# The normalised context in the expert layer transposed by block pairs on all 128 partitions, each tile stored as four pieces

## What is computed

```python
x = x + _L0_xattn_ref(_layernorm(x, axis=-1), ctx_512, ...)
x = x + _L0_ffn_ref(_layernorm(x, axis=-1), ...)   # 8 experts, all computed, weighted by the top 2
...
# _L0_ffn_ref
x1 = jnp.einsum('bsh,ehf->bsef', x, W1) + b1
x2 = jnp.einsum('bsh,ehf->bsef', x, W2) + b2
z = x1 * x2
g = jnp.einsum('bsef,efg->bseg', z, Wg) + bg
o = g * jax.nn.sigmoid(g) * (jnp.einsum('bsef,efg->bseg', z, Wl) + bl)
y = jnp.einsum('bsef,efh->bseh', o, W3) + b3
...
# layer 3, attention a2: the context is normalised over its 64 columns
yn = _ln(y, lny_g, lny_b)
```

## Time and profile before

| | us |
|---|---|
| median of 3 runs | 4445.98 (4444.93 to 4448.55) |
| the profiled execution, its own time | 4435.46 |
| its span in the profile | 4433.6 |
| share of the span: PE / DVE / ACT / POOL busy | 92% / 78% / 62% / 61% |

### The profile page before, as it was taken

One profiled execution on the slowest core, in us unless ns is written; L12 is line 12 of the kernel. 1 busy time (PEld: TensorE's weight loads), 2 busy tenths in 40 slices (PEclk: granted clock), 3 DMA queues, 4 the chain that ended last, 5 costly groups with the idle time before them and its releaser, 6 DMA issues. The chain is left out here.

```text
span 4433.6 us, 102799 instructions
## 1 busy us (share of the span) xinstructions
PE 4082.9 (92%) x40217; PEld 2922.3 (66%) x40217; DVE 3436.2 (78%) x6755; ACT 2732.0 (62%) x5298; POOL 2695.9 (61%) x2421
## 2 busy tenths in 40 slices
PE   7999999889988999999699999995996899999967
PEld 4777777655555777777557777774664577777754
DVE  6999998567778888888688888875554888888842
ACT  5777777534436777777467777771441677777721
POOL 3888788646674777777447777772002476777720
PEclk9999999889998999999699999995997999999975
DMA  4333333113331111111011111100000111111000
GB/s 113 90 94 94 89 95 89 47 62 114 112 98 58 54 37 54 39 52 38 19 44 53 37 54 45 45 30 18 1 1 28 43 46 45 50 49 45 30 12 9
DMA packets 107229, 236.66 MB, mean 53 GB/s; under 512 B 13496, under 2 KB 43464, under 8 KB 105368
## 3 DMA queue, kind: packets, MB, share of 16 engines
q1 hardware_dynamic: 106296, 230.03, 17.7%
q10 hardware_dynamic: 448, 0.06, 0.0%
HBM read 164.87 MB, written 50.26 MB: 49 GB/s over the span
## 5 line engine op out<-in xcount | busy, mean ns | idle before, releaser
L466 POOL TENSOR_TENSOR wst<-wst 125x384 bf16<-125x384 f32 (+1 forms) x1536 | 1632.6, 1063 | 833.0 <-ACT wst L664 768.3
L664 ACT ACTIVATE wst<-ps 125x448 f32<-125x448 f32 x3072 | 1498.5, 543 | 408.1 <-PE ps L164 399.1
L721 DVE TENSOR_TENSOR wst<-wst 125x512 bf16<-125x512 f32 (+1 forms) x1536 | 1404.0, 915 | 269.7 <-ACT wst L664 254.5
L164 PE MATMUL ps<-big,cx 128*125 128x448 bf16 (+1 forms) x6144 | 1435.5, 355 | 0.0
L164 PEld LDWEIGHTS ps<-cx,wst 125*128 125x128 bf16 x23040 | 1105.4, 98 | 354.4 <-issue 60.5
L164 PE MATMUL ps<-cx,wst 125*128 125x65 bf16 (+2 forms) x23040 | 1202.3, 204 | 27.5 <-POOL wst L466 13.3
L164 PEld LDWEIGHTS ps<-big,cx 128*125 128x125 bf16 (+1 forms) x6144 | 814.6, 137 | 287.4 <-issue 23.0
L164 PE MATMUL ps<-cx,big 128*128 128x500 bf16 (+1 forms) x2688 | 713.3, 318 | 27.8 <-DVE wst L691 15.0
L688 DVE CUSTOM_DVE_ANT_0 wst<-ps,wst 128x500 bf16<-128x500 f32 x896 | 603.7, 674 | 162.0 <-PE ps L164 122.8
L613 ACT ACTIVATE wst<-ps 128x500 bf16<-128x500 f32 x896 | 531.1, 593 | 221.9 <-PE ps L164 174.3
L691 DVE TENSOR_REDUCE wst<-ps 128x1 f32<-128x500 f32 x896 | 600.3, 670 | 36.1 <-PE ps L164 26.8
(11 more groups left out here) (203 smaller groups left out, 4232.7 us busy)
## 6 DMA issues: line engine op xcount, KB each, us to landing
cx<-ctxT SPq DMA_DIRECT2D x96, 375.0 KB, 3.5
cx<-ctxN SPq DMA_DIRECT2D x64, 377.9 KB
cx<-in_ctxN SPq DMA_DIRECT2D x64, 375.0 KB
cx<-ctxT SPq DMA_DIRECT2D x96, 187.5 KB, 3.8
ctxN<-cx SPq DMA_DIRECT2D x32, 377.9 KB
ynN<-cx SPq DMA_DIRECT2D x32, 377.9 KB
cx<-ynN SPq DMA_DIRECT2D x32, 377.9 KB
cTs<-in_ctxT SPq DMA_DIRECT2D x64, 187.5 KB, 6.8
```

Of the source, the lines that this page charges most:

```text
L164: return t.matmul(o, l, r, start=start, stop=stop, skip_group_check=True)
L466: g.tensor_tensor(pl[r][0:KP, at:], pf[r][0:KP, at:], pf[r][0:KP, at:].bitcast(BF16)[:, 1::2], ALU.subtract).then_inc(s["plp"], 1)
L664: e.activation(pf[T % 3][0:KP, cols], bank(2 + n2 % 3, 448)[0:KP], ACT.Exp, scale=scale).then_inc(s["ev"], 1)
L721: v.tensor_tensor(pl[r][0:KP, 0:to], pf[r][0:KP, 0:to], pf[r][0:KP, 0:to].bitcast(BF16)[:, 1::2], ALU.subtract).then_inc(s["pl"], 1)
```

## The change

Blocks i and i+6 of a batch are laid side by side in `ns` (`paired` gives the view in the old order). A pair is 128 columns wide, so one transpose puts block i on partitions 0 to 63 and block i+6 on partitions 64 to 127. A batch takes six transposes instead of twelve, three to a bank (375 columns), and two banks instead of three. ACT copies and DVE subtracts on all 128 partitions, two times 375 columns instead of three times 500. The tile in `cs` then holds the bf16 part in its first 750 columns and the rest in the other 750, with rows 0 to 749 of the batch on the lower and 750 to 1499 on the upper partitions; SP stores it into the unchanged layout of `yT2` as four transfers of 64 rows x 750 elements. What writes `ns` or reads it as rows (L1082, L1139, L914) does so through the paired view. The core of the diff; lines that only change a count of `ntl`, `ntm` or `stT` are left out:

```diff
+        def paired(v):
+            return v.rearrange("p (i h) c -> p h i c", h=2)
...
                 if 2 <= n <= B + 1:
-                    r += [("ntl", 3 * (n - 2) + g + 1) for g in range(3)]
+                    r += [("ntl", 2 * (n - 2) + g + 1) for g in range(2)]
...
-                    w.wait_ge(s["ntl"], 3 * b + 3)
-                    y.dma_start(yT2[b], cs[b % 3]).then_inc(s[f"stT_{b % 3}"], 16)
+                    w.wait_ge(s["ntl"], 2 * b + 2)
+                    for r in (0, 64):
+                        of = cs[b % 3][:, M // 2:] if r else cs[b % 3][:, 0:M // 2]
+                        y.dma_start(yT2[b][r:r + 64, 0:M // 2], of[0:64, :]).then_inc(s[f"stT_{b % 3}"], 16)
+                        y.dma_start(yT2[b][r:r + 64, M // 2:], of[64:128, :]).then_inc(s[f"stT_{b % 3}"], 16)
...
-                    g.tensor_tensor(o[:, :, C + 1:], ns[(b - 1) % 4], o[:, :, 0:C], ALU.subtract).then_inc(s["n5"], 1)
+                    o = o.rearrange("p (h i) c -> p h i c", h=2)
+                    g.tensor_tensor(o[:, :, :, C + 1:], paired(ns[(b - 1) % 4]), o[:, :, :, 0:C], ALU.subtract).then_inc(s["n5"], 1)
...
-                    for g in range(3):
+                    two = ns[b % 4].rearrange("p (i h) c -> p i (h c)", h=2)
+                    for g in range(2):
                         k = take()
                         w.wait_ge(s["n4"], b + 1)
-                        for i2 in range(4):
-                            r = t.transpose(bank(k)[0:64, KP * i2:KP * i2 + KP], ns[b % 4][:, 4 * g + i2, :], idf[0:KP, 0:KP])
+                        for i2 in range(3):
+                            r = t.transpose(bank(k)[:, KP * i2:KP * i2 + KP], two[:, 3 * g + i2], idf[0:KP, 0:KP])
                         r.then_inc(s["ntm"], 1)
...
-                    v.tensor_tensor(ns[u], cn[b % 2], q[:, 1, :].unsqueeze(2).broadcast_to([KP, KT, C]),
-                                    ALU.add).then_inc(s["n1"], 1)
+                    less = q[:, 1, :].rearrange("p (h i) -> p h i", h=2).unsqueeze(3).broadcast_to([KP, 2, KT // 2, C])
+                    v.tensor_tensor(paired(ns[u]), cn[b % 2].rearrange("p (h i) c -> p h i c", h=2), less, ALU.add).then_inc(s["n1"], 1)
...
-                        v.tensor_tensor(cs[b % 3][64:128, cols], bank(ffn_bank(at["norm", b] + g), 500)[0:64],
-                                        cs[b % 3][0:64, cols], ALU.subtract).then_inc(s["ntl"], 1)
+                        v.tensor_tensor(cs[b % 3][:, M // 2 + 375 * g:M // 2 + 375 * g + 375], bank(ffn_bank(at["norm", b] + g), 375),
+                                        cs[b % 3][:, 375 * g:375 * g + 375], ALU.subtract).then_inc(s["ntl"], 1)
...
-                    e.activation(cnb[b % 3][:, :, 0:C], ns[b % 4], ACT.Copy).then_inc(s["nbh"], 1)
-                    for g in range(3):
+                    e.activation(cnb[b % 3].rearrange("p (h i) c -> p h i c", h=2)[:, :, :, 0:C], paired(ns[b % 4]), ACT.Copy).then_inc(s["nbh"], 1)
+                    for g in range(2):
-                        e.activation(cs[b % 3][0:64, 500 * g:500 * g + 500], bank(ffn_bank(at["norm", b] + g), 500)[0:64],
+                        e.activation(cs[b % 3][:, 375 * g:375 * g + 375], bank(ffn_bank(at["norm", b] + g), 375),
```

More of the change, by code:

```diff
@@ L882, in wait_stored @@
                 w.wait_ge(s[f"stN_{i}"], 16 * third(i, B))
-                w.wait_ge(s[f"stT_{i}"], 16 * third(i, B))
+                w.wait_ge(s[f"stT_{i}"], 64 * third(i, B))
         def wait_split(w):
@@ L1004, in ffn_takes @@
                     at["norm", n - 2] = i
-                    i += 3
+                    i += 2
             return at
@@ L1079, in dve_f0 @@
                     if b >= 4:
-                        w.wait_ge(s["ntm"], 3 * (b - 3))
+                        w.wait_ge(s["ntm"], 2 * (b - 3))
                     w.wait_ge(s["n1"], 3 * b + 2)
-                    v.tensor_tensor(ns[u], cn[b % 2], q[:, 1, :].unsqueeze(2).broadcast_to([KP, KT, C]),
-                                    ALU.add).then_inc(s["n1"], 1)
+                    less = q[:, 1, :].rearrange("p (h i) -> p h i", h=2).unsqueeze(3).broadcast_to([KP, 2, KT // 2, C])
+                    v.tensor_tensor(paired(ns[u]), cn[b % 2].rearrange("p (h i) c -> p h i c", h=2), less, ALU.add).then_inc(s["n1"], 1)
                 if 1 <= n <= B:
@@ L1092, in dve_f0 @@
                     b = n - 2
-                    for g in range(3):
-                        cols = slice(500 * g, 500 * g + 500)
-                        w.wait_ge(s["nta"], 3 * b + g + 1)
-                        v.tensor_tensor(cs[b % 3][64:128, cols], bank(ffn_bank(at["norm", b] + g), 500)[0:64],
-                                        cs[b % 3][0:64, cols], ALU.subtract).then_inc(s["ntl"], 1)
+                    for g in range(2):
+                        w.wait_ge(s["nta"], 2 * b + g + 1)
+                        v.tensor_tensor(cs[b % 3][:, M // 2 + 375 * g:M // 2 + 375 * g + 375], bank(ffn_bank(at["norm", b] + g), 375),
+                                        cs[b % 3][:, 375 * g:375 * g + 375], ALU.subtract).then_inc(s["ntl"], 1)
         def act_f0(e, w):
@@ L1134, in act_f0 @@
                         w.wait_ge(s[f"stN_{b % 3}"], 16 * (b // 3))
-                        w.wait_ge(s[f"stT_{b % 3}"], 16 * (b // 3))
+                        w.wait_ge(s[f"stT_{b % 3}"], 64 * (b // 3))
                     else:
@@ L1138, in act_f0 @@
                     w.wait_ge(s["n4"], b + 1)
-                    e.activation(cnb[b % 3][:, :, 0:C], ns[b % 4], ACT.Copy).then_inc(s["nbh"], 1)
-                    for g in range(3):
-                        w.wait_ge(s["ntm"], 3 * b + g + 1)
-                        e.activation(cs[b % 3][0:64, 500 * g:500 * g + 500], bank(ffn_bank(at["norm", b] + g), 500)[0:64],
+                    e.activation(cnb[b % 3].rearrange("p (h i) c -> p h i c", h=2)[:, :, :, 0:C], paired(ns[b % 4]), ACT.Copy).then_inc(s["nbh"], 1)
+                    for g in range(2):
+                        w.wait_ge(s["ntm"], 2 * b + g + 1)
+                        e.activation(cs[b % 3][:, 375 * g:375 * g + 375], bank(ffn_bank(at["norm", b] + g), 375),
                                      ACT.Copy).then_inc(s["nta"], 1)
@@ L1147, in wait_f0 @@
             w.wait_ge(s["n5"], B)
-            w.wait_ge(s["ntl"], 3 * B)
+            w.wait_ge(s["ntl"], 2 * B)
         def pool_l1(g, w):
```

## The result

| | us |
|---|---|
| before, median of 5 runs | 4446.89 (4444.93 to 4448.55) |
| after, median of 5 runs | 4427.81 (4425.08 to 4432.47) |
| after / before | 0.9958, 95% interval 0.9944 to 0.9973 |
| profiled execution after: span, own time | 4426.5, 4428.29 |

4423.9 was forecast, in a range of 4409 to 4434.

A forecast was written before the change was run, and what follows sets the result against it. Taken as the bound: a one-step dependency circle of 12.69 us, not PE alone. 21.4 us from steps of 11.95 and 0.7 at the end make 22.1; 4445.98 - 22.1 = 4423.9, range 4409 to 4434.

The forecast's parts named there:

- The two circles: Expert loop of layer 0: a one-step dependency loop sets 12.69 us; one through POOL over two steps then sets 11.95.
- The stall of 0.60: PE's wait in each step before mid's second pair, ended by DVE's L1096; forecast to go with 11 takes.
- The circle over two steps: Down, DVE, POOL to transposes 14.20 us, then transposes, up, mid to a down 9.70: 23.90 for two periods.
- the rival of PE alone: Expert loop: POOL's latency does not bind, a step is PE's own 11.48 us, kernel 4411; chance 0.10.
- Transposes: On PE in each step: six wide ones take 0.67 us instead of twelve in 1.28, gain 0.61.
- the rival of bound loads: PE's transposes: weight loads are exposed, six take 1.15 to 1.28 us, kernel 4431 to 4433; chance 0.14.
- PE's wait for POOL: Before the transposes, for POOL's L909: 0.47 us a step on average, nearly none and 0.95 in turn.
- DVE and ACT: Expert loop: DVE subtracts 750 columns instead of 1500, about 0.8 us less a step; ACT copies as many fewer.
- the rival of the longer circle: L1082's paired write or another DVE instruction in the expert loop gets slower, gain vanishes, about 4438; chance 0.10.
- The end: Last two batches, up to layer 1's start: the stretch hangs on POOL and only shifts; shorter rounds give 0.7 us.
- Stores: SP issues four pieces instead of one, 0.34 us each; costed at nothing, in the loop and for the last store.
- The clock: Expert loop: PE's waits before transposes drop its clock; with 10% of steps at half clock, 4456; chance 0.04.

The follow-up runs named there:

- the two repetitions: Kernel before and changed kernel, each unchanged, run and profiled a second time: 4446.49 us, ratio 1.0002, and 4426.33 us, ratio 0.9959.
- the fourth pass: Changed kernel with one more POOL pass over each batch, ahead of the last one, result unused: 4470.68 us, ratio 1.0057 to the kernel before.
- the instructions alone: Changed kernel with a third bank taken per batch and left empty, so twelve takes a step again: 4444.31 us, ratio 0.9993 to the kernel before.
- the moved transposes: Kernel before, its twelve takes kept, with the transposes moved from behind down to behind up of the next step: 4467.49 us, ratio 1.0051.

## Why the prediction was right

**The two circles** (right). The stall of 0.60 before the second pair of mid went with the order of the banks, as forecast. The circle over two steps took its place: 14.21 + 9.69 = 23.90 in the trace, 14.20 + 9.70 = 23.90 in the prediction. With it the rival of PE alone falls, since PE waits for POOL. A POOL pass less brings PE's own 11.45. A pass more adds its length to two steps, but 1.5 us besides, by the clock in one circle and by the slowed difference in the other.

**Transposes** (right). 0.67 us for six. The weight loads last 146 ns on average and do not show in the spacing; the rival of bound loads falls.

**PE's wait for POOL** (size a bit off). 0.95 us was forecast in every second step. From down to the transposes it is 2.59 us in one and 1.94 in the other, 0.81 and 0.16 over down's own 1.78. The sum is as forecast, its split is less sharp.

**DVE and ACT** (right). L1103 545 ns and L1149 468 ns, forecast 0.5 and 0.45. DVE subtracts for 3 x 0.665 - 2 x 0.545 = 0.9 us less a step, forecast as about 0.8, off the circles. The difference through the paired view takes 959 ns as before, so the rival of the longer circle falls.

**The end** (right). L144 waits for L921, whose passes start as the last transposes do; with 22.1 us from the expert layer (22.3 in the two repetitions) the sum holds.

**Stores** (wrong). The step that failed is the store term: "SP issues four pieces instead of one, 0.34 us each", and behind it "I cost it at nothing, and the last store, too". The pieces take 0.45 to 0.60 us each, 2.4 us from the first piece to the rows (1106.88 to 1109.30). In the loop that stays covered, as said. Behind it the last batch's pieces and rows hold back layer 1's first loads, since SP waits for all stores before it issues them, and about 3 us are lost there. This is one of the signs that the prediction set for itself, that anything behind the expert loop changes its length. 22.1 - 3 is the 19.1 that the medians show; the agreement is closer than the runs' spread allows to claim, and so much of it is luck.

**The profiled execution.** The prediction set it 10.5 us under the median and subtracted from both alike. That was sound, and the runs show where most of the offset lies: the first profile is 17.6 us shorter than the repetition behind the loop, and 14.7 of them are in two stretches with another granted clock, far from the change. What makes the clock of such a stretch differ between executions of one program was not tried and stays open.

**The clock** (rival, right not to prefer). Behind its waits of 0.64 us PE paid nothing in the changed kernel; behind 2.5 us, with the fourth pass, it paid 1.54 every two steps. The kernel was then slower than before, but the clock was not the only cost in it.

## What to carry to other kernels

Look for circles that span more than one step: an engine that waits only in every second step, by twice as much, is bound by a latency that enters with half its length. And before adding or moving work, look at what it will meet: a pass of POOL for which the order had room cost 1.6 us a step, because DVE's instructions beside it got longer. Where buffers are taken in turn, a change in the number of takes, or in their order, reassigns every release; list for each take which engine releases it and what stands ahead of that release in its queue, since together with the shorter instructions this was worth 15 us here, against 7 for the instructions alone, and with the old takes the moved transposes lost 21 us. And compare stretches that contain the change, not spans: one of two profiled executions of the same kernel was 17.6 us shorter than the other in a part that the change had not touched.

## What the runs showed of the hardware

- A DVE addition of two float32 operands in SBUF, 0.96 us alone, took 2.37 us where it met a POOL pass, and ended 0.8 us after it. A DVE instruction on 125x12 elements, 0.17 us alone, took 0.69 us and ended with POOL's pass. Row sums (L1086 in the kernel with a fourth pass, one input) kept their 0.94 us beside POOL.
- Transfers of 64 rows x 750 elements take SP 0.45 to 0.60 us each to issue back to back, against 0.34 for one of 128 rows x 1500.
- Behind a wait of 2.5 us PE's granted clock was 0.50 over the next 3 us; behind one of 0.64 us six transposes took the same 0.67 us as behind none.
